# Expert bias added to the rows by an adding transfer instead of a TensorE product, and the low parts of the expert weights spread over the tiles

## The reference, cut to what matters

```python
def _L1_ffn_ref(x, gate_w, gate_b, expert_w, expert_b):
    xf = x.reshape(-1, x.shape[-1])
    gate_logits = xf @ gate_w.T + gate_b
    selected = jnp.argmax(jax.nn.softmax(gate_logits, axis=-1), axis=-1)
    out = jnp.zeros((xf.shape[0], expert_w.shape[1]), dtype=xf.dtype)
    for j in range(expert_w.shape[0]):
        yj = xf @ expert_w[j].T + expert_b[j]
        out = out + jnp.where((selected == j)[:, None], yj, 0.0)
    return out.reshape(*orig_shape[:-1], expert_w.shape[1])
...
x = x + jnp.tanh(g_ffn[1]) * _L1_ffn_ref(_layernorm(x, axis=-1), ...)
```

## Time and profile before

| | |
|---|---|
| median of three runs | 776.22 us (775.0 to 779.72) |
| profiled execution: device time | 775.54 us |
| profiled execution: span of the trace | 773.7 us |
| PE busy over the span | 743.4 us (96%) |
| DVE, ACT, POOL busy | 454.9, 429.2, 280.4 us |
| first tile's first product to the last one's end | 716.65 to 768.3 us |

### The profile page before, as it was taken

The page is one execution under the profiler, slowest core; times in us unless marked ns, Lnnn a source line. Parts: engine busy times, 40 slices in busy tenths (PEclk is TensorE's granted clock), DMA queues, the critical chain, the costliest instruction groups (busy, mean ns, idle before and its releaser), DMA issues.

```text
span 773.7 us, 12412 instructions
## 1 busy us (share of the span) xinstructions
PE 743.4 (96%) x3867; PEld 586.8 (76%) x3867; DVE 454.9 (59%) x1008; ACT 429.2 (55%) x1274; POOL 280.4 (36%) x440
## 2 busy tenths in 40 slices
PE   8999999999999999999999999999999997887997
PEld 7788887888787887878888878788787652565785
DVE  4796403646556556555555654656558764887652
ACT  4753327566556555556656555655655565656831
POOL 0531006344235235233424424523312458714233
PEclk9999999999999999999999999999999999997999
DMA  8545451502321041140140123103232144755142
GB/s 310 187 150 178 137 179 56 192 14 69 120 87 69 14 178 51 45 177 27 55 188 16 69 70 136 70 14 125 62 109 85 55 143 157 289 229 193 44 114 78
DMA packets 41230, 87.82 MB, mean 114 GB/s; under 512 B 5561, under 2 KB 26041, under 8 KB 37202
## 3 DMA queue, kind: packets, MB, share of 16 engines
q1 hardware_dynamic: 37924, 78.71, 29.2%
q0 software_dynamic: 3248, 8.41, 3.1%
HBM read 70.28 MB, written 35.57 MB: 137 GB/s over the span
## 4 chain that ended last, share of the span: by engine, by line
PE 84%; DVE 5%; POOL 3%; ACT 3%; DMA 3%; issue 2%; POOLq 0%; SPq 0%; DVEq 0%
PE banks L962 8%; PE banks L964 7%; PE banks L996 7%; PE banks L963 7%; PE banks L998 7%; PE banks L997 7%; PE banks L946 7%; PE banks L983 3%; PE banks L429 3%; PE banks L427 3%; PE banks L428 3%; PE banks L975 2%; PE banks L1923 2%; PE banks L1922 2%; PE banks L1921 2%; PE banks L1007 2%
## 5 line engine op out<-in xcount | busy, mean ns | idle before, releaser
L630 ACT ACTIVATE p_sb<-p_sb,nmax 128x128 f32<-128x128 f32 x256 | 99.7, 392 | 56.7 <-DVE nmax L850 56.7
L625 ACT ACTIVATE oT_hi<-banks 128x512 fp32r<-128x512 f32 x64 | 38.2, 597 | 132.3 <-PE banks L1009 132.3
L887 DVE SCALAR_TENSOR_TENSOR x_sb<-banks,tgates,x_sb 128x512 f32<-128x512 f32 x64 | 47.9, 748 | 62.8 <-PE banks L998 62.8
L742 POOL TENSOR_TENSOR v_lo<-v_raw,v_hi 128x128 fp32r<-128x128 f32 x64 | 29.5, 461 | 125.6 <-ACT v_hi L673 125.6
L845 DVE SCALAR_TENSOR_TENSOR p_sb<-banks,q_rstd,mask 128x128 f32<-128x128 f32 x256 | 71.5, 343 | 2.5 <-POOL q_rstd L83 2.4
L747 POOL TENSOR_TENSOR p_sb<-p_sb,rsum 128x512 f32<-128x512 f32 x64 | 66.7, 1041 | 15.1 <-DVE rsum L877 15.1
L946 PEld LDWEIGHTS banks<-kT,qT_sb 128*128 128x128 f32 x512 | 66.9, 191 | 5.4
L946 PE MATMUL banks<-kT,qT_sb 128*128 128x128 f32 x512 | 67.3, 274 | 0.0
L834 DVE TENSOR_TENSOR oT_lo<-banks,oT_hi 128x512 fp32r<-128x512 f32 x64 | 44.1, 689 | 32.0 <-ACT oT_hi L625 31.9
L877 DVE RECIPROCAL rsum<-prob_sum 128x4 f32<-128x4 f32 x64 | 11.3, 177 | 80.9 <-ACT p_sb L630 80.9
L881 DVE TENSOR_TENSOR pT_lo<-banks,pT_hi 128x512 fp32r<-128x512 f32 x64 | 44.2, 691 | 23.2 <-ACT pT_hi L648 23.2
(11 more groups left out here) (289 smaller groups left out, 1889.1 us busy)
## 6 DMA issues: line engine op xcount, KB each, us to landing
sorted_x<-in_empty SPq DMA_DIRECT2D x8, 2064.0 KB, 10.4
w_raw<-in_wq_l SPq DMA_DIRECT2D x8, 1024.0 KB, 5.7
w_raw<-in_wo_l SPq DMA_DIRECT2D x8, 1024.0 KB, 4.8
exp_w<-in_exp_w_l SPq DMA_DIRECT2D x8, 1024.0 KB, 9.5
kT_scr<-kT_st SPq DMA_DIRECT2D x16, 256.0 KB, 2.4
v_scr<-v_st SPq DMA_DIRECT2D x16, 256.0 KB, 2.5
xs<-sorted_x SPq DMA_DIRECT2D x15, 258.0 KB, 2.7
v_raw<-v_scr SPq DMA_DIRECT2D x14, 256.0 KB, 2.6
```

Of the source, the lines that this page charges most:

```text
L630: last = act.activation(p_sb[:, b % 2, h * P:(h + 1) * P], p_sb[:, b % 2, h * P:(h + 1) * P], ACT.Exp, bias=nmax[:, b % 2, h:h + 1], accum ...
L887: dve.scalar_tensor_tensor(out=s.x[:, b, :], in0=o_ps[b % 2][:, :], scalar=s.tgates[:, 0:1], in1=s.x[:, b, :], op0=ALU.mult, op1=ALU.add). ...
```

## The change

It does two things, both in the tile phase.

**The bias by a transfer.** In `attention` ACT now multiplies the bias by tanh(g) in one operation (`scale_bias`), and SP stores this one array of 8 rows to HBM (`d.bias`). `exp_b2`, its zeroing, its load and the product L1916 are gone; `start` moves to the first of the 12 products. In their place POOL issues for each tile an indirect transfer (`add_bias`) that fetches for each of the 128 rows the same row of `d.bias` (which one stands in `s.fixed`, a small table loaded with the gate's, or in `tile_i`) and adds it to `xs` in SBUF on the way. It waits for `xn_done`, since the normalisation must read the rows without the bias, and `add_y` waits for it (`bias_added`).

**The low parts spread.** The pieces are counted singly. ACT makes five experts' high parts ahead of the tiles instead of four, and then two pieces in each of tiles 0 to 5. DVE makes one expert's low parts (four pieces) in step 0 and two pieces in each of steps 1 to 6, after `add_y`.

```diff
@@ attention, scalar
-                    act.activation(s.exp_b_hi[:, :], s.exp_b[:, :], ACT.Copy).then_inc(s.exp_b_split, 1)
+                    act.activation(s.bias[:, :], s.exp_b[:, :], ACT.Identity, scale=s.tgates[0:E, 3:4]).then_inc(s.exp_b_scaled, 1)
@@ attention, sync
-            sp.wait_ge(s.exp_b_split, 2)
-            sp.dma_start(d.exp_b2[0], s.exp_b_hi[:, :].bitcast(F32)).then_inc(s.exp_b_stored, 16)
-            sp.dma_start(d.exp_b2[1], s.exp_b_lo[:, :].bitcast(F32)).then_inc(s.exp_b_stored, 16)
+            sp.wait_ge(s.exp_b_scaled, 1)
+            sp.dma_start(d.bias, s.bias[:, :]).then_inc(s.exp_b_stored, 16)
@@ experts, sync
-            sp.wait_ge(bias_zeroed, 1)
-            sp.dma_start(s.exp_b2[0:2, :, :].bitcast(F32), d.exp_b2).then_inc(exp_b_ld, 16)
@@ experts, scalar
             def split_w(n):
-                e = ORDER[n]
+                e, kt = ORDER[n // KT], n % KT
                 act.wait_ge(s.exp_ld[e // 2], 32)
-                for kt in range(KT):
-                    act.activation(s.ew_hi[:, e, kt, :], s.exp_w[:, e, kt, :], ACT.Copy).then_inc(w_hi_done, 1)
+                act.activation(s.ew_hi[:, e, kt, :], s.exp_w[:, e, kt, :], ACT.Copy).then_inc(w_hi_done, 1)
...
-            for n in range(READY):
+            for n in range((READY + 1) * KT):
                 split_w(n)
-            act.wait_ge(gateT_done, 2)
-            act.activation(s.exp_b2[:, :, :], s.zero[:, 0:1].unsqueeze(2).to_broadcast([P, E, D]), ACT.Copy)\
-                .then_inc(bias_zeroed, 1)
...
             def split_next_w(t):
-                if READY <= t < E:
-                    split_w(t)
-
-            run([(normalise, 2), (split_x, 1), (split_next_w, 3)])
+                for n in range((READY + 1) * KT + 2 * t, min((READY + 1) * KT + 2 * t + 2, E * KT)):
+                    split_w(n)
+
+            run([(normalise, 2), (split_x, 1), (split_next_w, 0)])
@@ experts, gpsimd
-            for t in range(TILES):
-                store(t)
+            def add_bias(t):
+                slot = t % SLOTS
+                pool.wait_ge(xn_done, t + 1)
+                if t == E:
+                    pool.wait_ge(tile_done, 1)
+                which = s.fixed[:, t:t + 1] if t < E else tile_i[:, t - E:t - E + 1]
+                pool.indirect_dma_start(out=xs[:, slot, 0:D], out_offset=None, in_=d.bias,
+                                        in_offset=IndirectOffsetOnAxis(ap=which, axis=0),
+                                        compute_op=ALU.add).then_inc(bias_added[slot], 16)
+
+            run([(add_bias, 2), (store, 0)])
@@ experts, vector
             def add_y(t):
                 slot = t % SLOTS
+                dve.wait_ge(bias_added[slot], 16 * (t // SLOTS + 1))
                 dve.wait_ge(y_done, t + 1)
...
             def split_next_w(t):
-                if READY <= t < E:
-                    split_w(t)
-
-            run([(split_x, 1), (add_y, -1), (split_next_w, 2)])
+                first = READY * KT + (2 * t + 2 if t else 0)
+                for n in range(first, min(first + (2 if t else KT), E * KT)):
+                    split_w(n)
+
+            run([(split_x, 1), (add_y, -1), (split_next_w, 0)])
@@ experts, tensor (multiply)
-                if t == 0:
-                    pe.wait_ge(exp_b_ld, 16)
-                pe.matmul(out, s.ones_r[:, :], s.exp_b2[:, e, :], start=True, stop=False)
                 for kt in range(KT):
                     if t < E:
                         pe.wait_ge(w_lo_done, KT * t + kt + 1)
                     cols = slice(kt * P, (kt + 1) * P)
-                    pe.matmul(out, xsT_hi[:, t % 2, cols], s.ew_hi[:, e, kt, :], start=False, stop=False)
+                    pe.matmul(out, xsT_hi[:, t % 2, cols], s.ew_hi[:, e, kt, :], start=(kt == 0), stop=False)
```

More of the change, by code:

```diff
@@ L51 @@
 NOWHERE = 1e9
-GATE_LOADS = 9
+GATE_LOADS = 10
 ARENA, SIDE = 144 * 1024, 28 * 1024
@@ L711, in copy_xT @@
                 if after(u, b, g, HB - 1):
-                    act.wait_ge(s.exp_b_stored, 32)
+                    act.wait_ge(s.exp_b_stored, 16)
                     for n in (0, 1, 2):
@@ L895, in x_stats @@
                         layernorm_var(dve, s, x_step, 2 * (b + 1), LN2_LAST[b]).then_inc(xval_done, 1)
[L897 to L901, removed]
             def copy_xT(u, b, g, odd):
                 if after(u, b, g, HB - 1):
-                    dve.wait_ge(s.exp_b_stored, 32)
+                    dve.wait_ge(s.exp_b_stored, 16)
                     for n in (3,):
@@ L1534, in experts @@
         w_hi_done, w_lo_done = m.sem("ew_hi_done"), m.sem("ew_lo_done")
-        exp_b_ld, bias_zeroed = m.sem("exp_b2_ld"), m.sem("bias_zeroed")
+        bias_added = [m.sem(f"bias_added{i}") for i in range(SLOTS)]
         y_done, res_done = m.sem("ey_done"), m.sem("eres_done")
@@ L1762, in split_w @@
             def split_w(n):
-                e = ORDER[n]
-                for kt in range(KT):
-                    dve.wait_ge(w_hi_done, KT * n + kt + 1)
-                    dve.tensor_tensor(s.ew_lo[:, e, kt, :], s.exp_w[:, e, kt, :], s.ew_hi[:, e, kt, :].bitcast(F32),
-                                      ALU.subtract).then_inc(w_lo_done, 1)
+                e, kt = ORDER[n // KT], n % KT
+                dve.wait_ge(w_hi_done, n + 1)
+                dve.tensor_tensor(s.ew_lo[:, e, kt, :], s.exp_w[:, e, kt, :], s.ew_hi[:, e, kt, :].bitcast(F32),
+                                  ALU.subtract).then_inc(w_lo_done, 1)
             dve.wait_ge(s.recycled, 1)
@@ L1806, in _ @@
             list_tiles()
-            for n in range(READY):
+            for n in range(READY * KT):
                 split_w(n)
@@ L1949, in flamingo @@
     d.fold, d.empty = a["fold"], a["empty"].rearrange("(p k) n -> p (k n)", p=P)
-    d.exp_b2 = nc.dram_tensor("exp_b2", (2, E, D), F32, kind="Internal").ap()
+    d.bias = nc.dram_tensor("exp_bias", (E, D), F32, kind="Internal").ap()
+    d.fixed = a["fixed"].to_broadcast([P, E])
     d.eid, d.base = a["iota"].to_broadcast([P, E]), a["base"].to_broadcast([P, E])
@@ L2004, in flamingo @@
         s.exp_b = s.at("exp_b", [E, D], 112)
-        s.exp_b_hi, s.exp_b_lo = s.at("exp_b_hi", [E, D], 114, F32R), s.at("exp_b_lo", [E, D], 116, F32R)
+        s.bias = s.at("exp_bias", [E, D], 114)
         s.recycled_flag, s.recycled = m.sb("recycled_flag", [P, 1]), m.sem("recycled")
@@ L2008, in flamingo @@
         s.filled, s.ones_set, s.exp_b_ld = m.sem("filled"), m.sem("ones_set"), m.sem("exp_b_ld")
[L2009 removed]
+        s.exp_b_scaled, s.exp_b_stored = m.sem("exp_b_scaled"), m.sem("exp_b_stored")
         s.ctx_nat_ld = m.sem("ctx_nat_ld")
@@ L2030, in flamingo @@
             s.ctx_res, s.xln3, s.prod = beside("ctx_res", [P, B, D], 0), beside("xln3", [P, HB, D], 16), beside("prod", [P, 2, D], 24)
-            s.exp_b2, s.xn = beside("exp_b2", [P, E, D], 0, F32R), beside("xn", [P, 2, D], 24)
+            s.xn = beside("xn", [P, 2, D], 24)
             s.x3T = [s.at(f"x3T{c}", [P, KT, HALF], 8 * c) for c in range(2)]
@@ L2077 @@
         "base": (T * np.arange(E, dtype=np.float32)).reshape(1, E),
+        "fixed": np.array(ORDER, np.int32).reshape(1, E),
         "extra_row": (P * np.arange(1, B, dtype=np.float32)).reshape(1, EXTRA),
```

12 lines of the change are left out of this document (6 added, 6 removed).

## The result

The change made the kernel slower. The median was 781.79 us (780.98 to 783.62, four executions) beside 776.01 us for the kernel before on the same chip: ratio 1.0073, 95% interval 1.0047 to 1.0099. The prediction was 773.2 (770.9 to 778.0): wrong in sign, and the measured time is above the range.

What follows compares the result with a forecast made beforehand. PE was taken to bound the tile phase, busy 48.58 of 48.65 us. Bias product -3.5 and slots' round +0.5 gave -3.0 us, so 773.2 us as median from 776.22; range for 8 in 10: 770.9 to 778.0.

Steps and rivals of the forecast that it cites:

- The bias product goes: PE, tile phase: 15 rows of the bias product at 0.2315 us each come off the path, 3.5 us won.
- The slots' round: Tile phase, store to reload of xs slots: chain 12.4 us against 13.3 of PE's work; two stalls of 0.25, 0.5 us lost.
- Rival A: Slots' round takes most of the gain back: stores landing in 5.0 us leave 1.1, median 775.1; 5.8 leaves nothing; chance 0.20.
- The adding transfers at zero: POOL and DMA, tile phase: rows of 0.97 to 1.5 us, landing hidden within 9.5 us by PE's work; cost zero.
- rival B: POOL becomes the bound: from 1.65 us per adding transfer a pair exceeds PE's tile; at 2.46, 780.1 us; chance 0.15.
- rival C: Adding transfers land later than 9.5 us, each us more paid twice; at 12 us 2.0 slower, 778.2; chance 0.05.
- The rule on GpSimd and VectorE: DVE's two-input pieces slow POOL's SBUF reads: up to six pairs at 2.46 us rows, 3.9 us slower; raises B only a little.
- The spread, "makes the gain possible": DVE, tile phase: two pieces per step take 2.5 us, under PE's 3.22; four would run 1.8 us late; cost zero.
- The rest, zero: SP's exp_b2 load, the start of tile 0 and the attention operations: no cost or gain.
- within 1%: Measured time within 1% (7.8 us) of the kernel before: chance 0.92; a larger gain 0.02, a larger loss 0.06.

Runs made afterwards that it cites:

- slots14: The changed kernel with fourteen slots of xs instead of six, so that only tile 14 reloads a slot; ratio 0.9963 to the kernel before.
- pool_pace: The changed kernel with POOL adding the bias itself, in four pieces per tile, instead of the adding transfers, six slots; ratio 0.9977 to the kernel before.
- transfer_only: The changed kernel with the low parts split as before, four pieces in a DVE step; ratio 1.0121 to the kernel before.
- add_distinct: The changed kernel with each adding transfer fetching 128 different rows of x instead of one bias row 128 times; ratio 1.0038 to the kernel before.
- no_last_adds: The changed kernel without the adding transfers of the last three tiles (12 to 14); one execution, 778.02 us.
- plain_transfer: The changed kernel with the fifteen transfers copying into a scratch tile instead of adding into xs; ratio 1.0014 to the kernel before.

## Why the prediction was wrong

*The bias product goes, -3.5:* right. By phases 3.2 us.

*The slots' round, +0.5:* **the step that failed.** By phases, 55.8 - 48.8 = 7.0 us (slots14 shows 5.4 of them as the round; its other 1.6 it loses at the last adding transfer) where before there were about 0.5 (52.5 - 3.2 - 48.8). The working had every link, in the right order, and set 13.3 us against 12.4, a margin of 0.9. But it priced the transfers in it at their duration before: 3.46 for store to reload, itself below the mean of 3.76, and 2.72 for the reload, with 1.2 more for a late landing. "New transfers share the DMA engines" stood there with 0.25 us a round behind it, and for two rounds, as if the nine reloads didn't delay each other. Nothing asked how much of those engines fifteen more transfers take. A share of 0.30 in the phase stood in the earlier trace rows; at the stores' price per byte (5.5 us for 2.01 MB) fifteen transfers of 0.26 MB take 10.8 us, and by that estimate it would have become 0.5. It became 0.70. Rival A, at 0.20, was this mechanism: it stretched the stores by 2.1 us for a gain of 1.1, and by 2.9 for none. In the round above the store's link was 2.6 longer than the term in the sum. A still fell short of the result: it left out the reload's 1.6 us, the DMA time of the adding transfers in every round, and that a late `xsT_lo` delays the `add_y` behind it.

*The adding transfers at zero:* wrong in two places. POOL's row was 1.56, just above the 0.97 to 1.5 taken, and the store after it 1.03 to 1.27, so that a pair needs 3.2 and not 2.5 us. That is as much as PE's tile, where rival B begins; pool_pace shows that it cost little. Landing was 5.0, far from the limit of 9.5 (rival C). But the limit counted from `xn`, for tile 12, and the last one was issued at 768.33, 4.1 us after its `xn` (763.46 + 0.81), behind the store of tile 11 in POOL's list. DVE waited 2.65 us for it, about 1 us of that beyond the last product's end (771.99 + 0.39).

*The rule on GpSimd and VectorE.* The row of 3.90 us beside four pieces in transfer_only, and store rows of 2.47 there, say that such a contention exists. With two pieces per step the changed kernel's adding rows in the phase stay at 1.54 to 1.57 and its stores at 1.27 or less, against the 2.46 that was weighed for six pairs; only the first adding row, at 714.93, beside the last of the sixteen pieces, took 2.24. The Trainium skill ("SBUF — State Buffer", section "Who interferes with whom") says that a VectorE instruction with two SBUF inputs contends with a GpSimd instruction that reads SBUF. transfer_only agrees, with the row of 3.90 us beside four such pieces, and the changed kernel nearly avoids it.

*The spread, "makes the gain possible":* right: DVE's steps hold two pieces in 1.28 us, and without it the kernel loses another 0.5 to 0.7%.

*The rest, zero:* wrong by the tail, +1.25 us, 15 transfers at 0.083. Nothing before the result showed it. The first tile also came later (717.56 against 715.90), but this is not the change: add_distinct and no_last_adds, the same program up to there, start it at 714.46 and 714.52.

*Sum by what was measured:* -3.2 + 6.5 (7.0 less the 0.5 that the round cost before) + 1.25 = +4.6 us, where the two comparisons give 3.6 and 5.7. The chance of 0.92 for "within 1%" was right, and the direction inside it was not.

## What to carry to other kernels

When a change moves work into transfers, add up what they take of the DMA engines in the stretch, and stretch every transfer on a round trip by it; here a round with 0.9 us of margin in 13.3 did not bear 1.65 us more of all 16 engines per tile. An indirect transfer was no cheap substitute for 0.23 us of TensorE here; the adding fitted on an engine that was idle, with one transfer for all tiles. Buffers in memory that has just come free took away such a round for nothing, but with the product in place they gained 0.2 us of phase, and with the bias added by POOL 2.0 (50.8 to 48.8).

## What the hardware did that was not expected

- A transfer that adds into SBUF held POOL for 1.56 us where a plain one took 0.95 to 0.99, and all 16 DMA engines for about 1.65 us against 0.95, for the same 256 KB. It used 144 packets against 80: from 712 us to the end q0 counts 3360 packets in the changed kernel, 2400 in plain_transfer and 1200 for the stores alone, with fifteen transfers each. Its landing took 5.0 us in the chain, and the stores' went from 2.9 us in the median to 3.4 beside them.
- Where the 128 rows come from (one or 128 places) made no difference that could be measured.
- The end of the program grew by 0.083 us per further indirect transfer.
- Between 655 and 665 us, far ahead of the change, TensorE was granted 0.50 (1.2 GHz) throughout in some executions and 1.00 (2.4 GHz) for half of the stretch or all of it in others, in programs that are the same up to there. Here after, and add_distinct:

```profile
655.00:660.00 5.00, 4.13 (x20) 4.17 (x21) 2.90 (x5) 0.00 (x0) 3.81 (x4) 0.50 0.57 197
660.00:665.00 5.00, 5.00 (x12) 2.90 (x13) 3.58 (x16) 0.60 (x1) 2.57 (x3) 0.50 0.39 116
```

```profile
655.00:660.00 5.00, 4.12 (x26) 4.15 (x26) 2.89 (x5) 0.00 (x0) 3.78 (x5) 0.66 0.54 179
660.00:665.00 5.00, 5.00 (x20) 2.49 (x19) 4.32 (x18) 2.66 (x6) 3.31 (x7) 1.00 0.40 124
```

PE had idled for 2.5 and 3.3 us between 650 and 655 in these two, so its idle time there doesn't tell which gets the lower clock. The first `xsT_lo` comes 3.1 us earlier in add_distinct (714.46 against 717.56); that all of this is the clock isn't shown, but it is nearly as much as the effect under study: compare phases, not spans.
